# Attention and top-2 experts on one core: q and k projected together, VectorE writing the repeated rows

## What is computed

```
q = einsum('mc,bcn->bmn', Wq, xf) + bq      # Wq, Wk: 32 x 256, xf: 4 x 256 x 1024
k = einsum('mc,bcn->bmn', Wk, xf) + bk
v = einsum('oc,bcn->bon', Wv, xf) + bv      # 256 x 256
wmat = softmax(einsum('bmi,bmj->bij', q, k), axis=-1)
x = alpha * einsum('bcj,bij->bci', v, wmat) + x
t = tokens(x); t = t + proxy_attention(layernorm(t)); t = t + top2_experts(layernorm(t))
```

## Time and profile before

| | us |
|---|---|
| median of 3 runs | 932.44 |
| lowest, highest | 926.41, 950.83 |
| span of the profiled execution, first to last instruction | 956.1 |
| TensorE matmul busy in it | 826.8 |
| VectorE busy | 547.5 |
| ScalarE busy | 349.8 |
| GpSimd busy | 411.9 |

### The profile page before, as it was taken

One profiled execution on the slowest core, in us unless ns is written; L12 is line 12 of the kernel. 1 busy time (PEld: TensorE's weight loads), 2 busy tenths in 40 slices (PEclk: granted clock), 3 DMA queues, 4 the chain that ended last, 5 costly groups with the idle time before them and its releaser, 6 DMA issues.

```text
span 956.1 us, 21491 instructions
## 1 busy us (share of the span) xinstructions
PE 826.8 (86%) x5273; PEld 714.2 (75%) x5274; DVE 547.5 (57%) x1074; ACT 349.8 (37%) x467; POOL 411.9 (43%) x460
## 2 busy tenths in 40 slices
PE   4998989896998988614999998989999899999993
PEld 3887879795665765312898987979888898899993
DVE  4687787884444554430665655655556466566662
ACT  2755656573233333101432332332333233333330
POOL 1474656453115554463343443443444343444322
PEclk9999999997568777655999999999999999999997
DMA  9475776821113221201144253352534424422221
GB/s 307 157 302 208 281 288 230 341 88 46 45 44 45 45 67 44 67 1 34 35 123 120 44 167 74 87 165 33 162 80 121 122 43 121 122 43 40 35 23 20
DMA packets 55423, 105.71 MB, mean 111 GB/s; under 512 B 17008, under 2 KB 46576, under 8 KB 52176
## 3 DMA queue, kind: packets, MB, share of 16 engines
q1 hardware_dynamic: 38784, 81.47, 24.2%
q0 software_dynamic: 15232, 18.43, 11.6%
q10 hardware_dynamic: 1360, 5.24, 1.4%
HBM read 317.92 MB, written 43.06 MB: 378 GB/s over the span
## 4 chain that ended last, share of the span: by engine, by line
SPq 21%; PE 12%; DMA 11%; issue 9%; DVE 0%; POOL 0%; ACT 0%; DVEq 0%; POOLq 0%
SPq L1106 14%; DMA wbuf<-wsplit 10%; SPq L1124 4%; SPq L1118 2%; PE ps_h L65 2%; PE ps_h L67 2%; PE ps_h L66 2%; PE ps_y L65 2%; PE ps_y L67 2%; PE ps_y L66 2%; PE ps_ht L1320 1%; DMA out_tok<-y,to_row 1%; SPq L59 1%; SPq L58 0%; PE ps_x L1293 0%
## 5 line engine op out<-in xcount | busy, mean ns | idle before, releaser
L1182 POOL DMA_INDIRECT out_tok<-y,to_row x68 | 110.6, 1626 | 175.2 <-DVE y L1252 144.9
L65 PE MATMUL ps_y<-wbuf,gl 128*128 x544 | 156.2, 287 | 15.8 <-DMA wbuf<-wsplit 13.5
L66 PE MATMUL ps_y<-wbuf,gh 128*128 x544 | 155.4, 286 | 0.0
L67 PE MATMUL ps_y<-wbuf,gh 128*128 x544 | 155.0, 285 | 0.0
L65 PE MATMUL ps_h<-wbuf,xtl 128*128 x272 | 114.0, 419 | 8.8 <-DMA wbuf<-wsplit 8.4
L65 PEld LDWEIGHTS ps_y<-wbuf,gl 128*128 128x128 f32 x544 | 103.8, 191 | 21.3 <-issue 18.5
L1210 ACT ACTIVATE xth<-ps_x 128x256 fp32r<-128x256 f32 x68 | 26.2, 385 | 239.4 <-PE ps_x L1293 239.4
L1224 ACT ACTIVATE g<-hb 128x1024 f32<-128x1024 f32 x68 | 72.1, 1060 | 104.5 <-DVE hb L1264 104.5
L1264 DVE TENSOR_TENSOR hb<-ps_ht,bias 128x1024 f32<-128x1024 f32 x68 | 83.3, 1225 | 46.3 <-issue 38.0
L67 PE MATMUL ps_h<-wbuf,xth 128*128 x272 | 109.0, 401 | 0.0
L66 PE MATMUL ps_h<-wbuf,xth 128*128 x272 | 108.4, 398 | 0.0
(11 more groups left out here) (184 smaller groups left out, 1751.5 us busy)
## 6 DMA issues: line engine op xcount, KB each, us to landing
wbuf<-wsplit SPq DMA_DIRECT2D x134, 2048.0 KB
wsplit<-wbuf SPq DMA_DIRECT2D x12, 2048.0 KB, 12.2
wraw<-in_w SPq DMA_DIRECT2D x16, 1024.0 KB, 7.4
xraw<-in_x_ch ACTq DMA_DIRECT2D x5, 1024.0 KB, 11.1
tok<-in_x_tok SPq DMA_DIRECT2D x1, 4096.0 KB, 17.0
out_tok<-tok SPq DMA_DIRECT2D x8, 512.0 KB
normed<-x SPq DMA_DIRECT2D x8, 512.0 KB, 2.9
records<-places SPq DMA_DIRECT2D x71, 1.0 KB, 1.7
```

The costliest lines, as they stand in the source:

```text
L65: eng.matmul(out, ll, rh, start=first, stop=False)
L66: eng.matmul(out, lh, rl, start=False, stop=False)
L67: return eng.matmul(out, lh, rh, start=False, stop=last)
L1182: pool.indirect_dma_start(out=out, out_offset=bass.IndirectOffsetOnAxis(ap=to_row[:, par:par + 1], axis=0), in_=y[:, par, :], in_offset=No ...
```

## The change

The weights of q and k are laid side by side as 64 columns. One project_qk per image computes both into partitions 0 to 63 of `ps_sc`, with 12 matmuls in place of 24. It stands in front of weigh(6). ScalarE's two activations take 32 partitions each from `ps_sc` (q at 0 to 31, k at 32 to 63). VectorE's `stack` now copies the 32 rows to their own place, copies them again into another block of 32 partitions, and writes the low rest from them into the third block: q's own, repeated and low blocks are 0, 2 and 1; k's are 1, 0 and 2. score(0) waits for `qk_full` of kind 1. The weight load is one DMA in place of two, and the splits of the weights go over 128 elements a partition in place of 384.

```diff
-        wq_raw = sb("wq_raw", [P, 2, KT, 3 * MID])
+        wq_raw = sb("wq_raw", [P, KT, 2 * MID])
...
-            for kind in range(2):
-                sp.dma_start(wq_raw[:, kind], wqk3[kind].rearrange("(k p) m -> p k m", p=P)).then_inc(wqk_in, 16)
+            sp.dma_start(wq_raw[:, :, :], wqk.rearrange("(k p) m -> p k m", p=P)).then_inc(wqk_in, 16)
...
             def whole_qk(b, kind):
-                act.wait_ge(qk_mm, done(b * 2 + kind))
+                act.wait_ge(qk_mm, done(b))
                 act.wait_ge(turned, done(b * IT - 2 + kind))
-                act.activation(qkf[:, kind], (ps_sc, ps_pt[0])[kind][0:3 * MID, :], ACT.Identity,
-                               bias=bqk[:, kind:kind + 1]).then_inc(qk_full, 1)
+                at = slice(kind * MID, (kind + 1) * MID)
+                act.activation(qkf[at, kind], ps_sc[at, :], ACT.Identity, bias=bqk[at, :]).then_inc(qk_full, 1)
...
                 dve.wait_ge(scored, done(b * IT - 1))
-                dve.tensor_copy(qk3[:, kind], qkf[:, kind]).then_inc(qk_hi, 1)
+                own, again, low = [slice(r * MID, (r + 1) * MID) for r in ((0, 2, 1), (1, 0, 2))[kind]]
+                dve.tensor_copy(qk3[own, kind], qkf[own, kind]).then_inc(qk_hi, 1)
+                dve.tensor_copy(qk3[again, kind], qkf[own, kind])
                 dve.wait_ge(qk_hi, done(b * 2 + kind))
-                at = slice(MID, 2 * MID) if kind == 0 else slice(2 * MID, 3 * MID)
-                dve.tensor_tensor(qk3[at, kind], qkf[at, kind], qk3[at, kind].bitcast(F32), ALU.subtract).then_inc(qk_ok, 1)
+                dve.tensor_tensor(qk3[low, kind], qkf[own, kind], qk3[own, kind].bitcast(F32), ALU.subtract).then_inc(qk_ok, 1)
...
-            def project_qk(b, kind):
-
-                if kind == 0:
-                    pe.wait_ge(x_split, b + 2)
-                    pe.wait_ge(exped, done(b * IT - 1))
-                else:
-                    pe.wait_ge(pt_ok, done(b * IT - 2))
-                dst = (ps_sc, ps_pt[0])[kind]
+            def project_qk(b):
+
+                pe.wait_ge(x_split, b + 2)
+                pe.wait_ge(exped, done(b * IT - 1))
                 for n in range(N // HALF):
                     cols = slice(n * HALF, (n + 1) * HALF)
                     for k in range(KT):
-                        last = mm3(pe, dst[0:3 * MID, cols], (wqh[:, kind, k], wql[:, kind, k]),
+                        last = mm3(pe, ps_sc[0:2 * MID, cols], (wqh[:, k], wql[:, k]),
                                    (xh[:, k, cols], xl[:, k, cols]), k == 0, k == KT - 1)
...
-                        pe.wait_ge(qk_full, done(b * 2))
+                        pe.wait_ge(qk_full, done(b * 2 + 1))
...
-                    if more and it >= IT - 2:
-                        project_qk(b + 1, it - (IT - 2))
+                    if more and it == IT - 2:
+                        project_qk(b + 1)
                     weigh(it)
 
-            project_qk(0, 0)
-            project_qk(0, 1)
+            project_qk(0)
```

More of the change, by code:

```diff
@@ L129, in chunk_tiles, with build @@
     return tok[:, :, :].rearrange("p (b c) d -> p b c d", b=B)[:, :, bass.ds(c, 1), :].rearrange("p b a d -> p b (a d)")
-def build(nc, x_ch, x_tok, wqk3, bqk3, wv_t, bv, alpha, proxy_t, gate_t, w1, b1_t, w2, b2, out):
+def build(nc, x_ch, x_tok, wqk, bqk_in, wv_t, bv, alpha, proxy_t, gate_t, w1, b1_t, w2, b2, out):
     wsplit = nc.dram_tensor("wsplit", [E, P, WROW], F32, kind="Internal").ap()
@@ L151, in build @@
         stage_a(nc, sem, tok, wbuf, ident, fixed, xraw, xn, norm1, record_out, wsplit, normed, places, proxy_t, gate_t,
-                x_ch, x_tok, wqk3, bqk3, wv_t, bv, alpha, w1, w2)
+                x_ch, x_tok, wqk, bqk_in, wv_t, bv, alpha, w1, w2)
         tabs = keep("tabs", [P, 6, TILES], I32)
@@ L159, in stage_a @@
 def stage_a(nc, sem, tok, wbuf, ident, fixed, xraw, xn, norm1, record_out, wsplit, normed, places, proxy_t, gate_t,
-            x_ch, x_tok, wqk3, bqk3, wv_t, bv, alpha, w1, w2):
+            x_ch, x_tok, wqk, bqk_in, wv_t, bv, alpha, w1, w2):
     with ExitStack() as ctx:
@@ L166, in stage_a @@
         xh, xl = sb("xh", [P, KT, N], F32R), sb("xl", [P, KT, N], F32R)
-        wq_raw = sb("wq_raw", [P, 2, KT, 3 * MID])
-        wqh, wql = sb("wqh", [P, 2, KT, 3 * MID], F32R), sb("wql", [P, 2, KT, 3 * MID], F32R)
-        bqk = sb("bqk", [3 * MID, 2])
+        wq_raw = sb("wq_raw", [P, KT, 2 * MID])
+        wqh, wql = sb("wqh", [P, KT, 2 * MID], F32R), sb("wql", [P, KT, 2 * MID], F32R)
+        bqk = sb("bqk", [2 * MID, 1])
         wv_raw = sb("wv_raw", [P, KT, C])
@@ L179, in stage_a @@
         prob = sb("prob", [P, 2, N])
-        qkf = prob[0:3 * MID]
+        qkf = prob[0:2 * MID]
         pth, ptl = sb("pth", [P, 2, IT, P], F32R), sb("ptl", [P, 2, IT, P], F32R)
@@ L213, in _ @@
         def _(sp):
-            for kind in range(2):
-                sp.dma_start(wq_raw[:, kind], wqk3[kind].rearrange("(k p) m -> p k m", p=P)).then_inc(wqk_in, 16)
-            sp.dma_start(bqk[:, :], bqk3).then_inc(consts, 16)
+            sp.dma_start(wq_raw[:, :, :], wqk.rearrange("(k p) m -> p k m", p=P)).then_inc(wqk_in, 16)
+            sp.dma_start(bqk[:, :], bqk_in).then_inc(consts, 16)
             sp.dma_start(wv_raw[:, :, :], wv_t.rearrange("(k p) m -> p k m", p=P)).then_inc(consts, 16)
@@ L412, in _ @@
                 dve.sem_inc(s, CREDIT)
-            dve.wait_ge(wqk_in, 32)
-            dve.tensor_copy(wqh[:, :, :, :], wq_raw[:, :, :, :]).then_inc(wsm_hi, 1)
+            dve.wait_ge(wqk_in, 16)
+            dve.tensor_copy(wqh[:, :, :], wq_raw[:, :, :]).then_inc(wsm_hi, 1)
             dve.wait_ge(wsm_hi, 1)
-            dve.tensor_tensor(wql[:, :, :, :], wq_raw[:, :, :, :], wqh[:, :, :, :].bitcast(F32), ALU.subtract).then_inc(wsm_ok, 1)
+            dve.tensor_tensor(wql[:, :, :], wq_raw[:, :, :], wqh[:, :, :].bitcast(F32), ALU.subtract).then_inc(wsm_ok, 1)
             for k in range(KT):
@@ L1350, in _ @@
             all_tiles(pe, run)
-INPUTS = ["x_ch", "x_tok", "wqk3", "bqk3", "wv_t", "bv", "alpha", "proxy_t", "gate_t", "w1", "b1_t", "w2", "b2"]
+INPUTS = ["x_ch", "x_tok", "wqk", "bqk_in", "wv_t", "bv", "alpha", "proxy_t", "gate_t", "w1", "b1_t", "w2", "b2"]
 def kernel(x, L0_conv_Wq, L0_conv_bq, L0_conv_Wk, L0_conv_bk, L0_conv_Wv, L0_conv_bv, L0_conv_alpha,
@@ L1366 @@
         "x_tok": flat.transpose(0, 2, 1).reshape(TOK, C),
-        "wqk3": np.stack([np.tile(wq.T, (1, 3)), np.tile(wk.T, (1, 3))]),
-        "bqk3": np.stack([np.tile(np.asarray(L0_conv_bq), 3), np.tile(np.asarray(L0_conv_bk), 3)], axis=1),
+        "wqk": np.concatenate([wq.T, wk.T], axis=1),
+        "bqk_in": np.concatenate([np.asarray(L0_conv_bq), np.asarray(L0_conv_bk)])[:, None],
         "wv_t": wv.T,
```

## The result

| | before | after |
|---|---|---|
| median, us | 939.9 (4 runs) | 960.7 (4 runs) |
| lowest, highest | 926.4, 950.8 | 952.2, 966.3 |
| span of the profiled execution | 956.1 | 964.5 |
| end of GpSimd's last L312 (L311 after), the end of the attention stage's own work | 220.7 | 236.1 |

The ratio is 1.032, with a 95% interval of 1.021 to 1.043: slower. (The ratios compare undisturbed runs only, so they need not be the quotient of the medians.) I had forecast 942 us, a loss of 1%. The time lies outside my range, and the ratio is three times mine. Two repetitions further down give about 1.01. Both statements need an explanation. (The text ahead of the prediction lets the attention stage end at about 216 us; by the mark used from here on, the end of GpSimd's last L312, it ended at 220.7.)

The account below looks back on a forecast made before the run. VectorE's stack, held by GpSimd, was taken to bound the hand-over between images. Removed matmuls 0, copies +4.6 and clock +5.2 gave +9.8 us on the median 932.44: 942 us, range 929 to 953.

Parts of the forecast that it names:

- What bounds the hand-over: Between images, TensorE idles 2.4 us until VectorE's subtraction releases the first score; VectorE was shut out by GpSimd's L312.
- Matmuls removed, worth 0: At each of three hand-overs, 12 fewer projection matmuls save about 2.7 us of TensorE, all going into idle time.
- the rival that TensorE's work was the bound: In the attention stage, all removed matmuls would count: -11.2 us, giving 921 us; chance 0.06.
- Copies, +1.44 per hand-over: In VectorE's stack, one added copy of 0.72 us per kind delays the first score; three hand-overs cost 4.3 us.
- +0.3 forecast: At the kernel's start, four copies and two subtractions on VectorE end at 22.6 us, 0.3 later than the first score before.
- The rival that a copy into other partitions is slow: In VectorE's stack, such a copy takes 1.22 us or more, not 0.72: 4 us more, 946 us; chance 0.08.
- Clock, +2.0 per hand-over: After TensorE's longer gaps the granted clock falls each time, costing 1.4 to 2.6 us each, taken as 2.0.
- The sum, +9.8: Over the attention stage, 4.6 us from VectorE's copies plus 5.2 us from the lower clock.
- "Images follow one another rigidly": In the attention stage, a slow front moves the end of the image by the same amount, as a 1.40 us difference shows.
- The base and the range: For the whole time, +9.8 us on the median 932.44; range 929 to 953, widened by the spread of shown runs.
- The rival "slower by over 2%": The low clock stays about 12 us at each of four image fronts: 955 us; chance 0.09.

Follow-up runs that it names:

- direct_alpha: Changed kernel with ScalarE writing both rounded blocks from PSUM, no VectorE copies, and alpha multiplied into v's weights and bias once at the start; ratio 0.987 to before.
- no_copy: Changed kernel without the second copy, its rows zeroed once at the start; ratio 1.004 to the kernel before, attention stage end at 224.1 us.
- direct: Changed kernel with ScalarE writing both rounded blocks from PSUM and VectorE doing one subtraction per kind, no copies; ratio 0.993 to before, stage end 217.0 us.
- filler24: Changed kernel with 24 unused matmuls behind weigh(7), filling TensorE's gap before the next first score; ratio 1.010 to before, stage end 223.4 us.
- again_after: The changed kernel once more, unchanged; ratio 1.012 to the kernel before, attention stage end at 230.5 us.
- third_after: The changed kernel unchanged, a third profile; no ratio on record, attention stage end at 230.9 us.
- again_before: The kernel before, unchanged, timed against itself; ratio 1.000, attention stage end at 218.8 us.
- third_before: The kernel before, unchanged, a third profile; ratio 0.999, attention stage end at 220.4 us.

## Why the prediction was wrong

- **What bounds the hand-over: right.** VectorE's stack, held by GpSimd. direct_alpha shows it by taking the hold away.
- **Matmuls removed, worth 0: right**, in three versions. no_copy also refutes the rival that TensorE's work was the bound.
- **Copies, +1.44 per hand-over: right**, 1.3 and 1.6 measured with the clock held; the second copy took 0.68 us, and it was held beside L311, which agrees with the exclusive lock of the Trainium skill ("SBUF — State Buffer", Who interferes with whom). L311 in its turn took 4.97 us with the first copy beside its start, and 4.57 in direct, which has no copies. At the start the first score came at 21.9, the same as before to within the spread of the first scores (+0.3 forecast). The rival that a copy into other partitions is slow did not come.
- **Clock, +2.0 per hand-over: right**, 2.0 measured with filler24 against again_after, 2.3 and 2.6 against third_after.
- **The sum, +9.8: near**, where no accident came in. Its parts by place (us, after less before, from the table above and the stage's end; rounded):

| | first vf | image 1 | image 2 | image 3 | behind the last hand-over | sum |
|---|---|---|---|---|---|---|
| forecast | 0.3 | 2.0 | 2.0 | 3.4 | 2.0 | 9.8 |
| first profiles | -0.5 | 1.9 | 1.7 | 9.8 | 2.4 | 15.4 |
| again_after, again_before | 0.8 | 3.0 | 2.0 | 3.5 | 2.3 | 11.7 |
| third_after, third_before | -0.8 | 2.4 | 2.6 | 3.7 | 2.6 | 10.5 |

The 3.0 of image 1 goes with again_before's clock, which held at 1.00 there. In each trace of the kernel before the clock fell at two of the four fronts, not always the same two; in each of the changed kernel at all four.
- **"Images follow one another rigidly": wrong.** This step failed: the delay was to be passed on from image to image at its own size. That holds only as long as VectorE meets GpSimd's instructions as before. In the first profile the clock's fall at 142 delayed the third image by 1.6 us (L307 starts 26.0 us after the first score in place of 24.4), and then L469 missed the change between two of GpSimd's instructions and cost another 4.5. That made 15.4 us out of 9.8. The trace before shows that L469 is held at all (it takes between 0.15 and 4.3 us there), and I did not count that as a risk; a hold over two instructions it does not show. That the later fall of the clock led to the missed change is not shown; why it was missed stays open.
- **The base and the range: wrong.** I placed the range by the spread of three runs (6 below, 18 above the median). With the four medians of the kernel before from the sessions of the experiments (938.9, 942.4, 943.1, 957.5, each on another chip), the scatter between sessions is as large as the effect. The shift of 20.8 between the medians of 4 runs is in part this scatter: the two repetitions give 8.3 and 11.7. The forecast of 942 stood on the median 932.4 of three runs; of four it is 939.9, which is 7.5 of the 18.7 us by which 960.7 missed it. The stage's 15.4 in place of 9.8, in the one run with a trace, is 5.6. How much of the first 3.2% was the accident and how much the clock of stage B stays open, since only one of those four runs has a trace. The rival "slower by over 2%" came true in this timing by its number alone: its mechanism, 12 us of low clock at each front, did not come, since in the three traces of the changed kernel the clock was back 4.5 to 6.2 us after the first scores.

## What to carry to other kernels

Before giving work to VectorE to relieve TensorE, look at which instruction releases the next matmul. If it is VectorE's own, fewer matmuls only turn into waiting, and a longer wait lowers the clock of what follows: here 24 useless matmuls in the gap made the stage 7 us shorter, by the traces; the whole times do not resolve it. Where VectorE is held by a long GpSimd instruction, look for every instruction of VectorE with copies or two inputs in SBUF that can fall under it, down to those of one element; the hold moves to the next one until all read from PSUM, go to ScalarE or are computed once beforehand. And where a kernel scatters by 3% between runs, read the end of the edited stage in the traces, and in more than one: it was steady to 2 us in the kernel before, where the whole time was not, but in the changed one it was 230.5, 230.9 and once 236.1.

## What I had not expected of the hardware

- VectorE does not always get in between two consecutive instructions of GpSimd: L469 did at 160.9 and did not at about 165.4 in the same image, waiting 6.23 us in place of some 1.7. It was the only miss at 36 such places in six traces.
- A gap before the first score lowered the clock at some hand-overs and not at others, in one program: in the kernel before, with 2.4 to 2.6 us, at four of nine; in direct, with 3.6 us, at two of three. With the changed kernel's 5.5 to 6.2 us it fell at all nine.
- Stage B, which no run edits, takes 195 to 225 us in the 18 traces, with its granted clock at 0.76 to 0.63; in the kernel before alone 197.5 to 220.8 us. Its TensorE was busy for 84 to 90% of the time in the four rows above.
